# Attention stage of a gated cross-attention and mixture-of-experts kernel: V kept as f32 words read as bf16 halves, a third bank for scores, one for the products of P with V

## What is computed

```
q = (layernorm(x) @ Wq) ; k = context @ Wk ; v = context @ Wv      # 16 heads of 16
attn = softmax(q k^T / 4)
x = x + tanh(g_xattn) * ((attn v) @ Wo)
xf = layernorm(x)
probs = softmax(xf @ router_w.T) ; keep the top 2, divide by their sum
h = silu(xf @ gate_w[e] + gate_b[e]) * (xf @ up_w[e] + up_b[e])
x = x + tanh(g_ffn) * sum_e probs[e] * (h @ down_w[e] + down_b[e])
```

## Time and profile before

| | |
|---|---|
| median of 3 runs | 587.91 us |
| the profiled execution: time, span | 587.68 us, 585.9 us |
| PE busy (share of the span) | 487.2 us (83%) |
| DVE busy | 427.8 us (73%) |
| ACT busy | 340.6 us (58%) |
| POOL busy | 290.4 us (50%) |
| granted TensorE clock, mean | 0.925 |
| attention block ends, experts block begins | about 339 us |

### The profile page before, as it was taken

One profiled execution on the slowest core, in us unless ns is written; L12 is line 12 of the kernel. 1 busy time (PEld: TensorE's weight loads), 2 busy tenths in 40 slices (PEclk: granted clock), 3 DMA queues, 4 the chain that ended last, 5 costly groups with the idle time before them and its releaser, 6 DMA issues. The chain is left out here.

```text
span 585.9 us, 15126 instructions
## 1 busy us (share of the span) xinstructions
PE 487.2 (83%) x4723; PEld 436.4 (74%) x4724; DVE 427.8 (73%) x902; ACT 340.6 (58%) x638; POOL 290.4 (50%) x252
## 2 busy tenths in 40 slices
PE   2988989999999999999989721699999999999920
PEld 2867888888888888888877621488889999999920
DVE  4865888999989989899999668488776555555410
ACT  4652557667667657766656591668665555554510
POOL 5092664545654555654456422506466756554440
PEclk9985999999999999999998955689999999999985
DMA  8565676665466465545331186748643434333333
GB/s 203 154 164 116 157 180 161 177 169 124 94 184 162 92 175 140 149 100 146 79 82 58 55 294 193 234 148 226 180 80 65 71 66 63 54 63 54 37 37 125
DMA packets 69022, 74.88 MB, mean 128 GB/s; under 512 B 28744, under 2 KB 57248, under 8 KB 68784
## 3 DMA queue, kind: packets, MB, share of 16 engines
q1 hardware_dynamic: 60912, 63.23, 40.3%
q0 software_dynamic: 8064, 11.06, 11.7%
HBM read 42.51 MB, written 14.98 MB: 98 GB/s over the span
## 5 line engine op out<-in xcount | busy, mean ns | idle before, releaser
L363 POOL TENSOR_TENSOR PL<-PT 125x448 f16<-125x448 f32 x96 | 100.5, 1049 | 131.5 <-ACT PT L496 131.5
L496 ACT ACTIVATE PT<-bank 125x448 f32<-125x448 f32 x192 | 104.0, 545 | 82.2 <-PE bank L633 81.3
L790 DVE TENSOR_REDUCE mx<-bank 112x1 f32<-112x375 f32 x256 | 130.7, 542 | 26.3 <-PE bank L615 24.5
L1248 POOL DMA_INDIRECT acc_scr<-ys,slot_row x42 | 67.0, 1595 | 82.6 <-ACT ys L1313 73.6
L615 PE MATMUL bank<-KS,QS 97*112 97x376 f32 x256 | 91.7, 380 | 12.5 <-DVE mx L790 11.5
L633 PE MATMUL bank<-QS,KS 98*125 98x256 f32 x384 | 82.9, 300 | 2.0 <-DMA QS<-nm 0.9
L1540 DVE SCALAR_TENSOR_TENSOR hf<-bank,ub,sg 128x256 f32<-128x256 f32 x84 | 38.5, 482 | 50.7 <-ACT sg L1290 50.6
L1378 PE MATMUL bank<-xH,GH 128*128 128x256 f16 x336 | 65.9, 278 | 6.4 <-issue 2.4
L633 PEld LDWEIGHTS bank<-QS,KS 98*125 98x125 f32 x384 | 65.9, 191 | 3.3 <-DMA QS<-nm 1.3
L1378 PE MATMUL bank<-xH,GL 128*128 128x256 f16 x336 | 65.7, 278 | 0.0
L1378 PE MATMUL bank<-xL,GH 128*128 128x256 f16 x336 | 65.6, 278 | 0.0
(11 more groups left out here) (215 smaller groups left out, 1083.7 us busy)
## 6 DMA issues: line engine op xcount, KB each, us to landing
KS<-kH SPq DMA_DIRECT2D x128, 94.0 KB, 2.2
KS<-kL SPq DMA_DIRECT2D x64, 94.0 KB, 2.2
QS<-q_scr SPq DMA_DIRECT2D x96, 56.0 KB
ctx_sb<-in_ctx SPq DMA_DIRECT2D x16, 281.2 KB
wsq<-in_L_ffn_gate_w SPq DMA_DIRECT2D x8, 512.0 KB, 3.9
wsq<-in_L_ffn_up_w SPq DMA_DIRECT2D x8, 512.0 KB, 4.6
w_raw<-in_L_ffn_gate_w SPq DMA_DIRECT2D x8, 512.0 KB, 4.5
w_raw<-in_L_ffn_up_w SPq DMA_DIRECT2D x8, 512.0 KB, 3.9
```

The lines of the kernel that those rows point to most:

```text
L363: pool.tensor_tensor(PL[:, 2 * k:2 * k + 2, :, 0:N], PT[:, 2 * k:2 * k + 2, :, 0:N], PH[:, 2 * k:2 * k + 2, :, 0:N], ALU.subtract).then_in ...
L496: act.activation(PT[:, 2 * k:2 * k + 2, :, 0:N].rearrange("p a e i -> p (a e) i"), psST[k % 2][0:JP].rearrange("p (a i) -> p a i", i=NI)[: ...
L790: dve.tensor_reduce(mx[:, hd:hd + 1], psS[hd % 2][0:N, 0:M], AX.X, ALU.max).then_inc(v_max, 1)
L1248: pool.indirect_dma_start(acc_scr, bass.IndirectOffsetOnAxis(ap=slot[:, TH * t + k:TH * t + k + 1].bitcast(U32), axis=0), ys[:, u, k, :], ...
```

## The change

- `VS` holds f32 words. ACT writes the projected V straight into its first 16 columns, in place of `vf` and the first bf16 copy; `VT` is a view of the upper bf16 halves of those words, at every second bf16 place, and is what PE reads. POOL forms the rests as `VS` minus `VT`, both from `VS`; ACT's second copy goes.
- The router's rows are centred once in the preparation (two instructions on DVE), so x needs no centring: DVE's `center` goes, ACT writes -x/256 in the pass that forms minus the mean, PE transposes that, and the scale is undone in ACT's copy. The variance is taken with the mean as a bias.
- Scores go round three banks (0, 1, 5). All products with V go to bank 4, so pair p4 (heads 8, 9) waits for DVE's reduction of heads 0 to 7 of the same batch.
- The slot tables change: seven `low` on POOL (slots 0, 1, 2, 3, 6, 7, 10), five on DVE; maxima transposed in slot 9; and others as below.
- `Wk`, `Wv`, `Wo` are loaded into room of `kL`.

```
-        psS, psST, psO = banks[0:2], banks[2:4], banks[4:6]
+        psS, psST, psO = [banks[0], banks[1], banks[5]], banks[2:4], banks[4:6]
-        VS = sb("VS", [JP, NB, JT, HEADS, VW], BF16)
+        VS = sb("VS", [JP, NB, JT, HEADS, VW], F32)
+        VT = VS[:].rearrange("p u t h w -> p (u t h w)").bitcast(BF16).rearrange(
+            "p (u t h w two) -> p u t h w two", u=NB, t=JT, h=HEADS, two=2)[:, :, :, :, :, 1]
-        POOL = [k for k in (1, 2, 3, 5, 6, 8) if k < SB]
+        POOL = [k for k in (0, 1, 2, 3, 6, 7, 10) if k < SB]
-        heads_at = {0: (0, 1), 1: (2, 3), 2: (4,), 3: (5, 6), 4: (7, 8), 5: (9, 10), 6: (11, 12), 7: (13, 14), 8: (15,)}
+        heads_at = {0: (0,), 1: (1, 2, 3), 2: (4, 5), 4: (6, 7), 5: (8, 9), 6: (10, 11), 7: (12, 13, 14), 8: (15,)}
-        VP = (4, 5, 6)
-        ST, AG, XC, XT, LG, RT = 5, 14, 7, 11, 12, 13
-        V1, VR, V2, LV = 3, 3, 6, 6
-        SQ = 4
-        MT, OT, OP, CT = 8, 9, 12, 10
+        VP = (5, 6, 7)
+        ST, AG, XT, LG, RT = 10, 12, 10, 12, 14
+        VR, LV = 2, 10
+        SQ = 7
+        MT, OT, OP, CT = 9, 9, 11, 9
...
-                    pool.tensor_tensor(head(vr), vf[:, u].rearrange("p t (h d) -> p t h d", d=HD), part(0), ALU.subtract).then_inc(g_r, 1)
+                    pool.tensor_tensor(VS[:, u, :, :, HD:2 * HD], VS[:, u, :, :, 0:HD], VT[:, u, :, :, 0:HD], ALU.subtract
+                                       ).then_inc(g_r, 1)
...
-                    act.activation(vf[:, u].rearrange("p t n -> p (t n)"), misc[0:JP, 0:JT * DIM], ACT.Copy
+                    act.activation(VS[:, u, :, :, 0:HD].rearrange("p t h d -> p (t h) d"),
+                                   misc[0:JP, 0:JT * DIM].rearrange("p (m d) -> p m d", d=HD), ACT.Copy
...
-                    wait(pe, v_max, HEADS * b + hd - 1)
-                    pe.matmul(psS[hd % 2][0:N, 0:MP], QS[u][0:RM, hd // 2, hd % 2, 0:N], KS[u][0:RM, hd // 2, :],
+                    wait(pe, v_max, HEADS * b + max(0, hd - SBANKS + 1))
+                    pe.matmul(psS[hd % SBANKS][0:N, 0:MP], QS[u][0:RM, hd // 2, hd % 2, 0:N], KS[u][0:RM, hd // 2, :],
...
                     if p % 4 == 0:
-                        wait(pe, v_os, 2 * (b - 1) + p // 4 + 1)
+                        wait(pe, v_os, 2 * b + p // 4)
-                                mm = pe.matmul(psO[hd // 8][:, VW * (hd % 8):VW * (hd % 8 + 1)], P[:, JT * p + t, e, :],
-                                               VS[:, u, t, hd, :], start=(part == 0 and t == 0),
+                                mm = pe.matmul(psO[0][:, VW * (hd % 8):VW * (hd % 8 + 1)], P[:, JT * p + t, e, :],
+                                               VT[:, u, t, hd, :], start=(part == 0 and t == 0),
...
-                    pe.wait_ge(v_xc, b + 1)
+                    pe.wait_ge(a_mean, b + 1)
...
+                dve.wait_ge(i_rw, 16)
+                dve.tensor_reduce(mx[0:E, 0:1], rw[:], AX.X, ALU.add).then_inc(v_rs, 1)
+                dve.wait_ge(v_rs, 1)
+                dve.scalar_tensor_tensor(out=rw[:], in0=mx[0:E, 0:1].to_broadcast([E, DIM]), scalar=-1.0 / DIM,
+                                         in1=rw[:], op0=ALU.mult, op1=ALU.add).then_inc(v_rm, 1)
```

More of the change, by code:

```diff
@@ L120, in attention @@
         first = lambda name, shape, dt: early.enter_context(nc.sbuf_tensor(name, shape, dt))
-        Wf = {k: first(f"w{k}_f", [p, 2, DIM], F32) for k, (_, p) in shapes.items()}
+        Wf = {k: f32(kL[0:shapes[k][1], n, :, 0:DIM]) for n, k in enumerate("kvo")}
+        Wf["q"] = first("wq_f", [128, 2, DIM], F32)
         mask_sb = first("mask_sb", [B, M], U8)
@@ L368, in values @@
                     b, h, u = at(i, c - 1)
[L369 to L372, removed]
-                    pool.tensor_tensor(head(vr), vf[:, u].rearrange("p t (h d) -> p t h d", d=HD), part(0), ALU.subtract).then_inc(g_r, 1)
+                    pool.wait_ge(a_V, b + 1)
+                    pool.tensor_tensor(VS[:, u, :, :, HD:2 * HD], VS[:, u, :, :, 0:HD], VT[:, u, :, :, 0:HD], ALU.subtract
+                                       ).then_inc(g_r, 1)
                 def last_values(i, c):
                     b, h, u = at(i, c - 1)
[L377 to L380, removed]
+                    pool.wait_ge(g_r, b + 1)
+                    pool.tensor_tensor(VS[:, u, :, :, 2 * HD:3 * HD], VS[:, u, :, :, HD:2 * HD], VT[:, u, :, :, HD:2 * HD],
+                                       ALU.subtract).then_inc(g_V, 1)
                 pool.memset(tg[:], 1.0).then_inc(s_one, 1)
@@ L454, in variances @@
                     act.wait_ge(p_xc, b + 1)
-                    act.activation(xc[:], xc[:], ACT.Square, scale=DIM ** -0.5,
+                    act.wait_ge(a_mean, b + 1)
+                    act.activation(xc[:], X[:, bass.ds(b, 1), :].rearrange("i o d -> i (o d)"), ACT.Square,
+                                   bias=mv2[:, bass.ds(b, 1), 0:1].rearrange("i o d -> i (o d)"),
                                    accum_out=mv2[:, bass.ds(b, 1), 1:2].rearrange("i o d -> i (o d)")
@@ L498, in slots @@
                                            ACT.Exp).then_inc(a_E, 1)
-                        if k == V1 and live(i, c, 1):
-                            b, h, u = at(i, c - 1)
-                            act.wait_ge(a_V, b + 1)
-                            wait(act, p_PV, PAIRS * (b - NB + 1))
-                            act.activation(VS[:, u, :, :, 0:HD].rearrange("p t h d -> p (t h) d"),
-                                           vf[:, u].rearrange("p t (h d) -> p (t h) d", d=HD), ACT.Copy).then_inc(a_V1, 1)
                         if k == KP[-1] and live(i, c, 0):
@@ L710, in slots @@
                             project_v(i, c, VP.index(s))
-                        for hd in heads[1:2]:
+                        for hd in heads[1:]:
                             scores(i, c, hd)
@@ L751, in _ @@
                 turn(0)
-                pe.wait_ge(i_rw, 16)
+                pe.wait_ge(v_rm, 1)
                 for k in range(2):
@@ L796, in normalise @@
                     hs = slice(8 * half, 8 * half + 8)
-                    o = psO[half][0:N, 0:8 * VW].rearrange("i (h w) -> i h w", w=VW)
+                    o = psO[0][0:N, 0:8 * VW].rearrange("i (h w) -> i h w", w=VW)
                     dve.reciprocal(rden[:, hs], o[:, :, VW - 1]).then_inc(v_rd, 1)
@@ L1408, in link @@
                     dve.wait_ge(e_r, n_chain[0])
-                dve.tensor_scalar(veps[:], mv2[:, :, 1], LN_EPS, None, ALU.add).then_inc(e_ve, 1)
+                dve.tensor_scalar(veps[:], mv2[:, :, 1], 1.0 / DIM, LN_EPS, ALU.mult, ALU.add).then_inc(e_ve, 1)
                 dve.wait_ge(s_sq, 1)
```

37 lines of the change are left out of this document (12 added, 25 removed).

## The result

The changed kernel takes 565.84 us (median of 4 runs, 560.17 to 567.23), the kernel before beside it 587.98: a ratio of 0.9605, 95% interval 0.9537 to 0.9674. The prediction was 565.3, range 557 to 579. The profiled execution took 564.71 us, its span is 562.9, against 587.68 and 585.9 before. PE is busy 84% of the span, DVE 73%, ACT 56%, POOL 53%.

What follows compares the result with a forecast made beforehand. It took DVE, nearly level with PE in a two-bank handshake, to bound the 17.7 us attention step. Twelve steps by 1.6 (19.2), 1.6, 0.8, 0.3 and 0.7 total 22.6 off 587.7: 565.1, stated as 565.3, range 557 to 579.

Steps and rivals of the forecast that it cites:

- DVE's work falls from 16.1 to 14.7: Attention step, DVE, the longer engine: centring (0.77 us) and one rest (0.62) leave it; a step becomes 14.7 plus 1.4 waits.
- the three banks: Score banks between PE and DVE: add no work, give back at most 1.1 us a step; 0.9 of waits kept.
- Centring, 0.77: DVE in each attention step: the centring goes, saving its mean duration of 0.77 us.
- One rest, 0.62: DVE in each attention step: one rest of twelve moves to POOL, saving DVE 0.62 us.
- p4's wait at nothing: PE in the step's tail: p4 waits 0.3 to 0.4 us for DVE's reduction, costed at nothing because PE leads.
- ACT bounds nothing: ACT in each attention step: two bf16 copies go, work falls from 11.9 to about 10.2 us, no bound on the step.
- SP: DMA issue of keys and maxima's row: floor of 15.6 us a step, some 15.2 with keys projected without a wait.
- Strided V at nothing: PE's 96 products a step: every-second-bf16 operand costs nothing; as rival, doubled pitch costs 2.6 us, 598 us, chance 0.07.
- The ends: Outside the full steps: first steps gain 0.3 us, the last centring at the end 0.7.
- Tail waits: Rival, step's tail: PE waits 0.6 to 1.0 us for POOL's rest or p4; step about 16.9, 575 us; chance 0.2.
- Both floors: Rival, attention step: third bank ends nearly every wait, a step is 15.3 and the time 555 us; chance 0.08.
- Work removed that turns into idle time: Rival, attention step: PE's order or SP's keys hold it; gain 0.2 to 0.6 a step, 580 to 585 us; chance 0.1.

Runs made afterwards that it cites:

- a_twobanks: Changed kernel with two banks for scores and two for the products with V again, new slot tables kept: 590.63 us, ratio to before 1.0100.
- a_tail_old: Changed kernel with the old slots of the tail (maxima transposed, context, output projection, centred rows, row means): 587.75 us, ratio to before 1.0045.
- b_words: Kernel before with only V held as f32 words read as bf16 halves, its slot tables kept: 587.62 us, ratio 1.0027.
- a_nowords: Changed kernel with V held as before (f32 copy, two bf16 copies by ACT): 571.47 us, ratio to before 0.9733.
- b_banks: Kernel before with only three banks for scores and one for products of P with V, its slot tables kept: 590.83 us, ratio 1.0084.
- a_heads_old: Changed kernel with the old places of the scores and of the values' projection: 579.52 us, ratio to before 0.9878.
- b_three: Kernel before with centring once, V as words and the new banks together, old slot tables and rests on POOL: 579.33 us, ratio 0.9872.

## Why the prediction was right, and where its reasons were not

**The size of a step, 16.1, came out at 16.03**, and the sum of 22.6 us at 22.1 (587.98 - 565.84). But the step that the prediction called its surest term, *DVE's work falls from 16.1 to 14.7*, does not carry the gain. Its number was right (14.8). Its weight was not: `a_twobanks` has the same DVE instructions as the changed kernel (DVE busy 15.3 a step) and is as slow as the kernel before.

**The term that failed is that of the three banks: "They can give back at most the 1.1 us a step that DVE waits for scores."** In the changed tables the third bank is worth 1.79 us a step (18.08 against 16.29); in the tables of before, alone, it costs 0.25. The bound was read from the waits of before, and those waits belonged to the order of before, which never puts three scores in a row. A bank, the tables and less work are one step, not three terms: with the old tables all three parts give 0.32, with two banks the tables and the other parts lose 0.24, and all together give 1.55. That the forecast was met rests on a sum that came out, DVE's work plus 1.4 of waits (measured in the turn: 1.33), and on this design reaching it, which the prediction assumed rather than derived. To that extent the close hit was luck.

Term by term:

- *Centring, 0.77.* Alone 0.24, off the step and off DVE's busy time. The rests grew from 616 to 685 ns at once. The mean duration from the earlier trace rows held 0.42 us of waiting for POOL, above the 343 ns of the instruction itself.
- *One rest, 0.62.* In DVE's favour, but DVE's remaining rests take 675 ns: 61 rests of 0.059 us more, 0.3 us a step. That, too, is waiting for POOL: the rests that are not held take 612 ns. So the 14.8 hold 0.3 us or more that is not DVE's work.
- *p4's wait at nothing.* Right: once, 0.5 us. The reason given, that PE leads by 0.5 and can afford 0.3 to 0.4, wasn't needed. The reduction started 0.70 us behind the transposition (forecast 0.71) and took 0.49, but PE's cover was 1.33 us (146.73 to 148.06), not 1.0: the transposition of the maxima itself, 0.20, was left out, the pair of `on` took 0.22 where 0.1 was put, and the pair of scores transposed 0.35 where 0.24 was put. `a_tail_old` shows how near that was: there the wait comes in every step, at 0.76.
- *ACT bounds nothing.* Right in the old order, wrong in the new one. ACT fell to 10.5, not 10.2. In the old order taking its copies away gave 0.31 a step in the turn (`b_words`), all of it the centring's wait for POOL. In the new one putting them back costs 0.52 (`a_nowords`), and there DVE waits for a late `oTH`.
- *POOL 10.6.* 10.1: the two V instructions take 1.47 and 1.85 us, before 1.65 and 1.71, and a rest 994 ns.
- *SP.* The floor of 15.6 was read too high: the 1.8 us of the earlier trace rows run from the issue of the DMA to its landing, so the 0.56 were counted twice, and it was 15.0. The row of maxima left at 148.10, 0.97 after it was written at 147.13, and in the twelve steps nothing waited for it. The bound of 15.2 wasn't reached. The other bound, 16.4 "if only DVE's removed work counts", is by the prediction's own terms 16.3 (17.7 less 1.4).
- *Strided V at nothing.* Right: 186 against 184 ns and 0.08 to 0.09 us for three. By the Trainium skill's figure for the moving operand's port (SBUF — State Buffer, section "SBUF: two separate sides") the step would be 1.3 us longer, as the prediction estimated from it; the runs don't bear that out here.
- *Preparation hidden.* Right; DVE still idled behind the two new instructions:

```profile
10.18 0.41 DVE L915 TENSOR_REDUCE mx<-rw 8x1 f32<-8x256 f32 x1 [0.69 <-DMA rw<-in_L_ffn_router_w]
10.62 0.41 DVE L917 SCALAR_TENSOR_TENSOR rw<-mx,rw 8x256 f32<-8x256 f32 x1
12.22 0.69 DVE L864 SCALAR_TENSOR_TENSOR wk_l<-kL,wk_h 96x512 fp32r<-96x512 f32 x1 [1.19 <-ACT wk_h L505]
```

- *The ends.* The first steps and the end were put at 3.4 us together, with the extra 1.6 and 0.8 steps. The `nm` of batch 0 gave 5.0 and the rest took 2.1 back, most of it where the clock was lower.

**The rivals.** Tail waits: not in this kernel (in the twelve steps no wait of PE for POOL's rests is listed), but they are what `a_tail_old` is. Its second half, the price of 0.6 us for a meeting of rests, was real but elsewhere: DVE's rests of the changed kernel are held up to 0.34 us in the twelve steps, and the step came out at 16.0 all the same. Both floors: no. Strided V: no. Work removed that turns into idle time: this is what happens with two banks, or with the old tables, and it was given only 0.1.

**What stays open.** Why the old tables with three banks lose behind the transposition (`b_banks`, 0.54 there) is argued from the waits and not tested. The new tables were reset in two groups, not number by number, and `a_heads_old` and `a_tail_old` together lose more (1.02 + 1.41) than all tables at once (`b_three`, 1.23), so they aren't independent either.

## What to carry to other kernels

Between two engines that pass tiles through a few banks, the time one waits for the other bounds what a bank is worth only for the order in which it was measured: a third bank allows an order with three tiles in a row, and the order is where its value lies. Test such a change by taking single parts back out of the new kernel as well as by putting them into the old one; here each part looked small from the old side, the bank even harmful, and each that was taken back out (bank, words, places of the scores, tail) cost 0.52 us a step or more. And before the mean duration of an instruction is booked as a saving, look at its minimum, and at what the other engines do when it is longer: what lies above the minimum may be a wait that its neighbours inherit, and busy time holds it.

## What the runs showed of the hardware

- A DVE rest that starts while a POOL instruction runs can be held until that one ends. In the traces of all 14 kernels, 258 of the 1184 rests on DVE took over 640 ns, and every one of them ends 0.476 to 0.484 us after a POOL instruction does; the others took 601 to 635 ns. The centring, too, ended 0.15 us after POOL's instruction whenever it took more than 360 ns. DVE's maxima, which read a bank, are not held: in the changed kernel they take 539 ns in the mean with a POOL instruction running, 537 without. It is a wait and not a slower rate, since the end keeps its distance from POOL's end whatever the overlap.
- The Trainium skill (SBUF — State Buffer, "Who interferes with whom") says that a DVE instruction with two SBUF inputs and a GpSimd instruction that reads SBUF contend, and that whoever has the shared ports keeps them for its whole instruction. DVE's rests have two such inputs, and their ends agree with it.
- A moving operand of bf16 at every second place streamed like a dense one at 49 columns: 186 ns against 184 in the median, and 0.08 to 0.09 us from start to start of three.
- The clock's low stretches fall otherwise from run to run, and one kernel's time with them: 560.2 to 567.2 us for the changed kernel, 579.5 to 592.8 in 31 runs of the kernel before. In the profile of `b_words` four of twelve steps hold such a stretch, and their mean is 17.80 us where the turn at full clock has 17.53.
